# Stores and reloads of the split weights issued by ScalarE instead of SyncE in a decoder layer on one core

## The reference

```python
x = _layernorm(x + attention(x, Wq, bq, Wk, bk, Wv, bv, Wo, bo))   # 16 heads of 128, 4 key heads, rotary, causal
x = _layernorm(x + wkv(w, u, x, ctx_2048))                         # a scan over the 256 tokens
x = _layernorm(x + moe_ffn(x, W, bias, rw1, rb1, rw2, rb2, A, B, gates))  # dense plus top-2 low-rank experts
```

## Time and profile before

| | us |
|---|---|
| median of 3 runs | 1857.01 (1853.22 to 1861.23) |
| profiled execution | 1865.38 |
| its span, first to last instruction | 1863.6 |
| mean granted TensorE clock | 0.962 of full speed |

### The profile page before, as it was taken

How to read it: one execution, slowest core, us unless ns; L and a number is a source line. 1 busy time by engine, 2 the same in 40 slices (tenths; PEclk the granted TensorE clock), 3 DMA queues, 4 the chain that set the end, 5 groups by cost and what they waited for, 6 DMA issues and landing times. The chain is left out here.

```text
span 1863.6 us, 36120 instructions
## 1 busy us (share of the span) xinstructions
PE 1679.0 (90%) x11648; PEld 1528.0 (82%) x11648; DVE 1612.3 (87%) x3953; ACT 1069.2 (57%) x2994; POOL 914.3 (49%) x889
## 2 busy tenths in 40 slices
PE   5899989998989898989998989899999884789998
PEld 4788988897989897988898889898888873677786
DVE  4666799899999999898999998989999988799887
ACT  4677766666666666666676666666666662121111
POOL 2333465547564655555546555655566544133221
PEclk8899999999999999999999999999999996889999
DMA  7565335223532353225312531254124412111211
GB/s 239 191 211 173 112 96 169 87 66 103 168 94 65 94 171 103 64 82 168 117 52 84 176 120 52 74 173 132 54 73 152 143 57 74 57 46 68 80 69 46
DMA packets 108554, 202.95 MB, mean 109 GB/s; under 512 B 16848, under 2 KB 58320, under 8 KB 108368
## 3 DMA queue, kind: packets, MB, share of 16 engines
q1 hardware_dynamic: 108368, 200.65, 33.6%
HBM read 120.89 MB, written 37.75 MB: 85 GB/s over the span
## 5 line engine op out<-in xcount | busy, mean ns | idle before, releaser
L759 POOL TENSOR_TENSOR RC<-QB,Cos 128x256 f32<-128x256 f32 x320 | 261.2, 816 | 577.5 <-DMA SW<-QB 476.1
L427 PE MATMUL bank<-Xh,W 128*128 128x256 f32 x1344 | 384.9, 286 | 38.1 <-DVE Xl L1035 26.4
L429 PE MATMUL bank<-Xh,W 128*128 128x256 f32 x1344 | 380.1, 283 | 0.0
L428 PE MATMUL bank<-Xl,W 128*128 128x256 f32 x1344 | 379.6, 282 | 0.0
L647 ACT ACTIVATE S<-S,NM 128x128 f32<-128x128 f32 (+1 forms) x512 | 229.0, 448 | 146.6 <-DVE NM L871 145.8
L427 PEld LDWEIGHTS bank<-Xh,W 128*128 128x128 f32 x1344 | 258.7, 192 | 41.7 <-DVE Xl L1035 30.3
L760 POOL TENSOR_TENSOR RSN<-SW,Sin 128x256 f32<-128x256 f32 x320 | 272.9, 853 | 0.0
L429 PEld LDWEIGHTS bank<-Xh,W 128*128 128x128 f32 x1344 | 259.4, 193 | 0.0
L428 PEld LDWEIGHTS bank<-Xl,W 128*128 128x128 f32 x1344 | 258.6, 192 | 0.0
L616 ACT ACTIVATE S<-S,RL 128x128 f32<-128x128 f32 (+1 forms) x512 | 203.6, 447 | 41.2 <-DVE RL L901 39.4
L427 PE MATMUL bank<-PTh,Vh 128*128 128x256 f32 (+1 forms) x512 | 138.1, 270 | 92.3 <-DVE OTl L866 91.9
(11 more groups left out here) (136 smaller groups left out, 4779.6 us busy)
## 6 DMA issues: line engine op xcount, KB each, us to landing
W<-kept SPq DMA_DIRECT2D x140, 512.0 KB, 3.6
SW<-QB SPq DMA_DIRECT2D x640, 64.0 KB, 2.0
kept<-W SPq DMA_DIRECT2D x40, 512.0 KB, 3.8
KVT<-in_wraw SPq DMA_DIRECT2D x40, 256.0 KB, 3.5
XR<-in_xt SPq DMA_DIRECT2D x16, 512.0 KB, 4.3
RO<-in_xn SPq DMA_DIRECT2D x16, 512.0 KB, 3.5
KVT<-in_ctxt SPq DMA_DIRECT2D x16, 512.0 KB, 5.0
mixed<-RO SPq DMA_DIRECT2D x16, 512.0 KB, 4.0
```

The source lines that it names most:

```text
L427: nc.tensor.matmul(dst, lhs[0], rhs[0], start=first, stop=False)
L428: nc.tensor.matmul(dst, lhs[0], rhs[1], start=False, stop=False)
L429: return nc.tensor.matmul(dst, lhs[1], rhs[0], start=False, stop=last)
L759: gp.tensor_tensor(RC[:, r % 2, :], QB[:, r % 2, :], Cos[:, :], ALU.mult)
```

## The change

In SyncE's `slot`, the two loops that issue the stores and the reloads go. The same loops, with the same waits and the same semaphores, stand at the end of ScalarE's `slot`, behind the two S copies and `tail(n, 1)`. They use ScalarE's DMA queue. Slots, tables, transfers and bytes are unchanged; only issuer, queue and place among the neighbours differ. For the first use of a half this puts a store ahead of the W copy of the same slot.

```diff
--- before.py
+++ after.py
@@ -361,18 +361,6 @@
                     if b >= 4:
                         sp.wait_ge(x2_out[ro_buf(b)], x2_stored(b - 4))
                     sp.dma_start(RO[:, ro_buf(b), :, :], xn[b, :, :].rearrange("(a p) c -> p a c", p=P)).then_inc(n_in[ro_buf(b)], 16)
-
-                for hf in range(HALVES):
-                    for i in range(NP):
-                        if KEEP_AT[i] + hf * HEADS * SWITCH[0] == n:
-                            sp.wait_ge(w_lo, hf * NP + i + 1)
-                            sp.dma_start(kept[hf, i, :, :], W[:, i, :, :].rearrange("p a n -> p (a n)").bitcast(fp32)).then_inc(w_kept[i], 16)
-                for at in SWITCH[1:]:
-                    for i in range(NP):
-                        if RELOAD_AT[i] + HEADS * at == n:
-                            piece_unused(sp, at, i)
-                            sp.wait_ge(w_kept[i], 16 * HALVES)
-                            sp.dma_start(W[:, i, :, :].rearrange("p a n -> p (a n)").bitcast(fp32), kept[SEQ[at][0], i, :, :]).then_inc(w_in[i], 16)
                 tau = tail_of(n, 2)
                 if tau is not None:
                     above(sp, ev_done, tau)
@@ -676,6 +664,18 @@
                     copy(S[:, i, P:P + T], S[:, i, P:P + T], scale=RL[:, i, 1:2]).then_inc(normed, 1)
                 tail(n, 1)
 
+                for hf in range(HALVES):
+                    for i in range(NP):
+                        if KEEP_AT[i] + hf * HEADS * SWITCH[0] == n:
+                            act.wait_ge(w_lo, hf * NP + i + 1)
+                            nc.scalar.dma_start(kept[hf, i, :, :], W[:, i, :, :].rearrange("p a n -> p (a n)").bitcast(fp32)).then_inc(w_kept[i], 16)
+                for at in SWITCH[1:]:
+                    for i in range(NP):
+                        if RELOAD_AT[i] + HEADS * at == n:
+                            piece_unused(act, at, i)
+                            act.wait_ge(w_kept[i], 16 * HALVES)
+                            nc.scalar.dma_start(W[:, i, :, :].rearrange("p a n -> p (a n)").bitcast(fp32), kept[SEQ[at][0], i, :, :]).then_inc(w_in[i], 16)
+
             def tail(n, part):
                 def at(lag, p):
                     return tail_of(n, lag) if part == p else None
```

## The result

The changed kernel takes 1889.19 us (median of 4 runs, 1886.23 to 1894.85), the kernel before 1859.12 beside it (4 runs). The ratio is 1.0164, 95% interval 1.0119 to 1.0208: slower by some 30 us, where 1860 was forecast and 1880 was the top of the range. The profiled execution took 1886.23 us. It is the shortest of its four, and the profiled one before lay 8.4 us above its median; so the two traces are 20.8 us apart, and what follows accounts for these 20.8, not for all 30.

A forecast was written before the change was run, and what follows sets the result against it. No engine was full; ScalarE's stretch from S copies to W copy was on the path early in the run. The terms -1 + 3.1 + 1 gave +3 us, 1860 against the median 1857.01; the range was 1851 to 1880.

The forecast's parts named there:

- rival 1: ScalarE stops 0.53 to 0.58 us at each DMA issue, in series: 1880 us, between 1872 and 1883; chance 0.26.
- 17.5 us in the slots with stores: 30 stores sharing a slot with a split, each costing ScalarE 0.58 us if nothing hides the issue.
- term of 3.1 us: Early slots where two or three stores share a slot with a split: issue time not hidden, 3.1 us in total.
- the cover: 0.69 us from ScalarE's S copies to its W copy, taken to hide a DMA issue that begins with the S copies.
- 1 us for double reloads: Steady-part slots with two reloads, 21 in all, overrun the hidden time on ScalarE; 1 us booked in total.
- Waits at 0: The waits `w_lo`, `piece_unused` and `w_kept`, moved to ScalarE, were taken not to block it: 0 us.
- Rival 2: SyncE and ScalarE take turns issuing, so stores wait for swap issues: 1863 to 1879 us, some 1866; chance 0.15.
- What is removed: 180 issues leave SyncE, 97.6 us of its time; VectorE gains at most 2.9 us, booked as 1 us.
- 2.9 us of the earlier trace: VectorE's idle time waiting for GpSimd's product, 5 times; used as the most that VectorE could gain.
- Rival 3: Faster: reloads on SyncE might cost 1.6 us per cycle, 11 us in all, giving 1846 us; chance 0.07.

The follow-up runs named there:

- stores alone: Changed kernel with the 140 reloads put back on SyncE, so ScalarE issues only the 40 stores; 1.0002 of the kernel before.
- half-size: Changed kernel with each reload cut to the high parts, 256 KB instead of 512 KB, same issues, places and waits; 1.0000 of the kernel before.
- early kernel: Changed kernel with each reload issued earlier in the same slot, right behind PTh, some 3 us ahead of the swap; 0.9996 of the kernel before.
- reloads alone: Changed kernel with the 40 stores put back on SyncE, so ScalarE issues only the 140 reloads; 1.0181 of the kernel before.

## Why the prediction was wrong

**What was right.** That one issue in a slot, and nearly all of the 180, cost ScalarE nothing. I gave the forecast 0.52 and rival 1 0.26. Rival 1's 1880 is not far from the measured time, but by another cause: its 17.5 us in the slots with stores did not come (1.0002 with the stores alone). The sequencer runs ahead, further than I took it to: the issue starts with the release of the S copies, not with their start. The rule of the Trainium skill ("TensorE: Matmul & The Clock Gate", section "Architectural detail: the array is 16× 32×32, not 1× 128×128") of a queue of 8 instructions in front of ScalarE agrees with the issues at 160.25 and 160.62, before OTh (160.28) and the S copies (160.63) that stand ahead of them have begun.

In the term of 3.1 us the double stores were too dear: 0.48 over the cover was booked, and the W copy stays at 0.69. The triple stores were about right: 1.06 each was booked, and 0.82 and 0.95 were measured in slots 13 and 14. Neither this nor the 1 us for double reloads can be seen in the whole time. Waits at 0: no loss came from them, since the half-size and early kernels have the same waits on ScalarE.

Rival 2 did not come about: ScalarE's issue at 160.62 begins inside the swap's of 160.40 to 160.87. Single ones are stretched (0.45 us here, and the second swap issue at 160.91, 0.94 us), but the first swap of a pair began inside an issue of ScalarE's 43 times, and its issue then took 0.461 us in the median, 0.462 otherwise. By the lock in the Trainium skill ("Perfetto Trace Analysis", section "DMA Instruction — HWDGE (DVE, Sync)") one issue would wait for the generator while another uses it, and this wait would stand inside its profiled length. The trace agrees at most in single cases: the swap issue of 160.40 began 0.18 us before the store's ended and is no longer than usual (0.47), the one of 160.91 is. One slip in that rival's sum: even odds between 1863 and 1879 give 1871, not 1866.

**The step that failed** is in "What is removed". I wrote that the swap rarely waits for the store behind it, and booked the change of order as a gain of 1 us at most. It took the order in SyncE's queue to be a burden on the swaps and did not see it as their protection: a reload right behind the swaps (the middle one 1.2 us behind the first, as the store in the earlier trace rows) has some 3.9 us up to the next ones to itself. The very running ahead on which the forecast rested puts ScalarE's issue where its last wait ends, near QB's end and so beside the swaps. The same fact that made the issue free made the transfer collide. I even had the moment: rival 2 places the store at 167.8, in the middle of the swap issues, but prices there only the issue, 0.58 us, and lets GpSimd's idle time take it. Of the moved step I costed the instruction and not its bytes on the DMA engines: the collision with the swap stood at nothing, and it measured a swap landing in 3.0 us instead of 2.0 in the median and 30 us in all, 1.0181 with the reloads alone.

**The 2.9 us of the earlier trace rows** I used as a bound from both sides. It bounds what earlier swaps can give, not what later ones cost. The prediction's first paragraph calls GpSimd's wait for the swaps "a wait with nobody behind it". Margin was not looked up: how long before RF starts GpSimd is done. With a swap a microsecond late in the median and up to 5.1 us to landing, RF took 39 us more of VectorE's time in the steady part, Ql 17 less, and the stretch grew by 19. The prediction's own sign of being wrong, that RF begins to wait for GpSimd, is what came.

**What I should have weighed** is a rule of the Trainium skill that speaks against the change, in "DMA: Bandwidth & Descriptors", section "Issuing engines are not separate DMA queues": transfers from all issuers run on the same 16 DMA engines and mix, and issuing from a second one saves only the issuer's time. The trace agrees: 33.6% of those engines' time in one queue, 33.8% in two, and swaps of one queue that land later beside reloads of the other. It would have raised the question of who now mixes with whom.

Rival 3 (faster) rested on the difference between the halves of a cycle. It was read from one cycle; over all cycles of before the halves take 94.6 and 94.4 us, so the earlier trace rows alone could not carry it. Nothing of it appeared, and the early kernel, where SyncE issues no store or reload, is no faster either. None of the versions beats the kernel before.

## What to carry to other kernels

When a transfer moves to another engine's queue, ask when it will be issued and not where it stands in the code: the issuer runs ahead to the last wait that holds it, and that can be the same event which releases a small, urgent transfer. Keep large transfers right behind the urgent one, with time up to the next, or about their own landing time ahead of it; a queue of its own does not part them. For a wait that is near zero, look up its margin before it is used as a bound on a loss.

## What the runs showed of the hardware

- A DMA issue on ScalarE took 0.327 us in the median and ran ahead of arithmetic in the program: 0.69 us from S copies to W copy with one or two issues in between, as without, and a ratio of 1.0000 with 140 reloads of 256 KB and 40 stores issued by it. With three issues in between it was 1.51 and 1.64 us.
- A pair of 64 KB swaps took 2.6 us from first issue to last landing, 4.0 with a 512 KB load issued within a microsecond ahead of it, and 5.2 with one issued between its two, from another queue.
- The same reload's issue took 0.530 us behind two swaps on SyncE and 0.33 us as the first in line, on SyncE and on ScalarE alike.
- 180 transfers of 16 bytes per partition, 2 KB each, cost 13 us in all, and beside them 512 KB reloads landed in 4.9 us instead of 3.6.
- A VectorE sum of 0.42 us took 2.38 us when a GpSimd product had started 0.07 us before it.
